# Three gathers to a PSUM bank, twelve places for gathered rows, steps of six, and fewer reports from TensorE

## What is computed

```
xn = layernorm(x)
W[r] = sum_b comp[r, b] * basis[b]                      # 8 relations, 4 bases
agg[dst] += xn[src] @ W[type]                            # over all edges
h = gelu(agg + xn @ loop_w + h_bias + xn)
gnn = layernorm(h) * gamma + beta
query, key = xn @ W_qk + b_qk;  value = xn @ W_v + b_v
lam = softmax(key over nodes)^T @ value;  mix = query @ batchnorm(lam)
x = x + gnn + mix
t = layernorm(x); e = argmax(t @ router_w^T + router_b)  # one of 32 experts
x = x + relu(relu(t @ W1[e] + b1[e]) @ W2[e] + b2[e])
```

## Time and profile before

| | us |
|---|---|
| median of 3 runs (lowest, highest) | 764.96 (764.16, 765.04) |
| profiled execution, its own time | 765.41 |
| its span, first to last instruction | 763.7 |
| mean granted TensorE clock | 0.903 of full |

### The profile page before, as it was taken

One profiled execution on the slowest core, in us unless ns is written; L12 is line 12 of the kernel. 1 busy time (PEld: TensorE's weight loads), 2 busy tenths in 40 slices (PEclk: granted clock), 3 DMA queues, 4 the chain that ended last, 5 costly groups with the idle time before them and its releaser, 6 DMA issues.

```text
span 763.7 us, 10470 instructions
## 1 busy us (share of the span) xinstructions
PE 602.2 (79%) x3189; PEld 474.0 (62%) x3189; DVE 381.1 (50%) x1267; ACT 167.1 (22%) x358; POOL 469.2 (61%) x480
## 2 busy tenths in 40 slices
PE   2577777888888877799999889987998895178980
PEld 1466666666666556676777668766867763166860
DVE  6534444223333324526566645657466566723652
ACT  3800000000000001102332312323223144135420
POOL 9667666666666666766666766677676600263265
PEclk9989996899999997699999989998999897579986
DMA  6643333332323334333444433444434316563021
GB/s 213 203 127 90 93 92 91 94 92 84 96 87 96 88 96 138 112 96 106 129 120 123 130 111 110 122 122 123 118 108 128 112 50 191 129 183 92 22 85 67
DMA packets 41873, 85.35 MB, mean 112 GB/s; under 512 B 11280, under 2 KB 23506, under 8 KB 41619
## 3 DMA queue, kind: packets, MB, share of 16 engines
q0 software_dynamic: 22576, 61.01, 27.4%
q1 hardware_dynamic: 18372, 22.95, 9.5%
q10 hardware_dynamic: 864, 0.65, 0.3%
HBM read 71.77 MB, written 12.80 MB: 111 GB/s over the span
## 4 chain that ended last, share of the span: by engine, by line
PE 43%; issue 16%; DVE 10%; POOL 10%; DMA 8%; another core or an unknown queue 5%; ACT 5%; DVEq 0%; ACTq 0%; POOLq 0%; SPq 0%
PE ps L846 22%; PE ps L904 7%; POOL gath L585 6%; DMA gath<-xn_d,src_i 5%; PE ps L893 3%; PE ps L873 2%; PE ps L1106 2%; POOL both L612 2%; DVE wmat L1241 2%; PE ps L1115 2%; POOL out L617 2%; DVE acc_raw L1265 1%; DMA both<-rows_d,inv_i 1%; PE ps L927 1%
## 5 line engine op out<-in xcount | busy, mean ns | idle before, releaser
L585 POOL DMA_INDIRECT gath<-xn_d,src_i x392 | 389.6, 994 | 191.0 <-issue 93.4
L846 PE MATMUL ps<-wmat,gath 128*128 128x144 f32 x1568 | 275.0, 315 | 53.3 <-DMA gath<-xn_d,src_i 25.6
L846 PEld LDWEIGHTS ps<-wmat,gath 128*128 128x128 f32 x1568 | 234.3, 206 | 93.0 <-issue 40.0
L1265 DVE TENSOR_TENSOR acc_raw<-acc_raw,ps 128x144 f32 x392 | 101.6, 300 | 276.4 <-PE ps L846 176.8
L1241 DVE TENSOR_TENSOR wmat<-hit,wts 128x576 f32<-128x576 f32 x100 | 75.3, 753 | 0.1
L612 POOL DMA_INDIRECT both<-rows_d,inv_i x25 | 24.3, 972 | 61.2 <-DVE inv_i L1514 49.1
L904 PE MATMUL ps<-wq_wv,acc_raw 128*128 128x256 f32 (+1 forms) x200 | 53.9, 389 | 2.8 <-issue 2.8
L904 PE MATMUL ps<-wk_et,acc_raw 128*128 128x256 f32 (+1 forms) x200 | 53.7, 392 | 0.9 <-issue 0.4
L893 PE MATMUL ps<-cmat,both 128*128 128x512 f32 (+1 forms) x100 | 47.2, 594 | 1.2 <-issue 1.1
L1560 DVE SCALAR_TENSOR_TENSOR acc_raw<-ps,wts,acc_raw 128x256 f32 x56 | 27.0, 482 | 41.2 <-PE ps L1115 28.6
L617 POOL DMA_INDIRECT out<-acc_raw,inv_i x25 | 25.8, 1032 | 34.2 <-DVE acc_raw L1551 28.1
(11 more groups left out here) (202 smaller groups left out, 616.7 us busy)
## 6 DMA issues: line engine op xcount, KB each, us to landing
gath<-xn_d,src_i POOLq DMA_INDIRECT x392
rows_d<-both SPq DMA_DIRECT2D x24, 256.0 KB
both<-in_x SPq DMA_DIRECT2D x24, 128.0 KB
both<-in_x SPq DMA_DIRECT2D x4, 640.0 KB, 9.8
xn_d<-both SPq DMA_DIRECT2D x4, 640.0 KB
acc_raw<-in_w_t SPq DMA_DIRECT2D x1, 2080.0 KB
acc_raw<-in_w_t SPq DMA_DIRECT2D x1, 2048.0 KB, 7.5
both<-in_x SPq DMA_DIRECT2D x1, 512.0 KB
```

Source lines behind the costliest of these rows:

```text
L585: g.indirect_dma_start(gath[:, k, :], None, xn_d, bass.IndirectOffsetOnAxis(ap=src_i[:, OCT * q + k:OCT * q + k + 1], axis=0)).then_inc(ga ...
L846: ins = t_.matmul(ps_edge[quarter][:, m * B * WIN:(m + 1) * B * WIN], gath[:, k, m * P:(m + 1) * P], wmat[:, k, :, :].rearrange("p b w -> ...
L1265: d.tensor_tensor(place, place, ps_edge[w][:, m * B * WIN:(m + 1) * B * WIN].rearrange("p (b w) -> p b w", w=WIN), ALU.add).then_inc(added, 1)
```

## The change

- A step ("sextet") has six columns in two triples instead of eight in four pairs; there are 65 steps (the last has seven columns) instead of 49. `gath` and `wmat` have RING = 12 places instead of 8.
- A triple has a whole PSUM bank: 8 groups (2 halves x 4 bases) of SPAN = 64 nodes. Each column keeps its own window of WIN = 22 nodes, at its own offset in the span. PE first clears the bank with a matmul of 512 bf16 columns of zeros, then each of the 3 x 2 products adds 4 runs of 22 numbers at an offset that PE has in a register (a register load for each step). DVE adds the whole bank, 512 columns, in one instruction for a triple.
- PE reports once for a triple (adding 3), once for both halves of a maximum, once for two keys, and once in all for the weighted sums.
- The table of bounds has bases of columns, offsets, bases of triples and a flag; it is stored in one transfer and loaded by four, `base_bc` in runs of six numbers for each partition. DVE computes it with about ten small operations.
- `STARTS` and the pieces' places in a step are laid out anew: two pieces after each triple. `ones_pp` and `reach` are made later.

```diff
-WIN = 36
-PAIR = 2
-OCT = 8
-NOCT = -(-E // (P * OCT))
-ETAB = (NOCT + 1) * OCT
+WIN = 22
+SPAN = 64
+THREE = 3
+SIX = 2 * THREE
+RING = 2 * SIX
+COLS = -(-E // P)
+NSIX = COLS // SIX
+NTRI = -(-COLS // THREE)
+ETAB = 432
-STARTS = [24, 25, 26, 27, 28, 29, 30, 31, 32, 34, 35, 36, 37, 38, 39, 40, 42, 43, 44, 45, 46, 47, 48]
+STARTS = [24, 25, 26, 28, 31, 34, 36, 39, 41, 43, 45, 47, 49, 50, 52, 54, 55, 57, 58, 60, 62, 63, 64]
...
-            sp.dma_start(base_bc, bounds_d[0:1, :].to_broadcast([P, NWIN])).then_inc(bounds_loaded, 16)
+            sp.dma_start(bounds_d, bounds[:, :]).then_inc(bounds_stored, 16)
+            sp.wait_ge(bounds_stored, 16)
+                sp.dma_start(base_bc.rearrange("p (r g) -> p r g", g=SIX),
+                              bounds_d[:, 0:SIX].rearrange("(a r) g -> a r g", a=1).to_broadcast([P, ROWS, SIX])).then_inc(bounds_loaded, 16)
...
+            def sextet(q, beside, i):
+                for c in [c for t3 in triples_of(q) for c in columns_of(t3)]:
+                    pool.wait_ge(multiplied, SIX + max(c - RING + 1, 0))
+                    g.indirect_dma_start(gath[:, c % RING, :], None, xn_d,
+                                         bass.IndirectOffsetOnAxis(ap=src_i[:, c:c + 1], axis=0)).then_inc(gathered[c % RING], 16)
...
+            def edges(t3, offsets):
+                bank = ps_edge[t3 % 4]
+                pe.wait_ge(added, t3 + 1)
+                t_.matmul(bank[:, :], onesb[0:1, :], identb[0:1, 1:2].to_broadcast([1, KD * B * SPAN]), start=True, stop=True)
+                pe.wait_ge(wmat_built, t3 + 1)
+                for c in columns_of(t3):
+                    pe.wait_ge(gathered[c % RING], 16 * (c // RING + 1))
+                    for m in range(KD):
+                        place = bank[:, :].rearrange("p (c n) -> p c n", n=SPAN)[:, m * B:(m + 1) * B, ds(offsets[c - THREE * t3], WIN)]
+                        ins = t_.matmul(place, gath[:, c % RING, m * P:(m + 1) * P], wmat[:, c % RING, :, :],
+                                        start=False, stop=True, skip_group_check=True)
+                ins.then_inc(multiplied, len(columns_of(t3)))
...
-                ins.then_inc(max_mult, 1)
+                if m == KD - 1:
+                    ins.then_inc(max_mult, KD)
...
-                t_.matmul(ps_mix[t % 2][0:n, 0:D], onesb[0:3, 0:n], shift3[:, :], start=False, stop=True).then_inc(keyed, 1)
+                if nth % 2 == 1:
+                    ins.then_inc(keyed, min(nth, 2))
...
-                ins.then_inc(summed, 1)
+                if nth == NT:
+                    ins.then_inc(summed, 1)
...
+                offsets = row_values(pe, off_row[0:1, cols[0]:cols[-1] + 1], SPAN - WIN, AN_OFFSET)
+                edges(2 * q, offsets[0:THREE])
+                piece(q, 0, beside, i)
+                piece(q, 1, beside, i)
+                edges(2 * q + 1, offsets[THREE:SIX])
...
+            def add_triple(t3, base):
+                v.wait_ge(multiplied, SIX + columns_of(t3)[-1] + 1)
+                v.wait_ge(added, t3 + 4)
+                place = acc[:, :, ds(base, SPAN)]
+                d.tensor_tensor(place, place, ps_edge[t3 % 4][:, :].rearrange("p (c n) -> p c n", n=SPAN), ALU.add).then_inc(added, 1)
```

More of the change, by code:

```diff
@@ L61 @@
 CLAMPED = "the pairs' experts and tiles are counts from zero, cut to the last expert and tile by a minimum before they are stored"
-A_NODE = "each base is the least node number among its edges, and acc has a row's width of columns beyond the last node"
+A_NODE = "each base is the least node number among its edges, and acc has a span of columns beyond the last node"
+AN_OFFSET = "each offset is a node number less the least of its triple, cut by a minimum to the last that leaves a gather's columns in the span"
 assert TS * TG == P and TS * TW == TC * P and KD * B * NPAD % ZEROS == 0
-assert OCT == 4 * PAIR and ETAB % ROWG == 0 and NT % GROUPS == 0 and PAIRS % 2 == 0
-assert STARTS[0] == CHAIN0 and len(STEP) == INLINE and INLINE == NT - 2 and STARTS[-1] == NOCT - 1
+assert NTRI == 2 * NSIX + 1 and ETAB % SIX == 0 and ETAB >= NTRI * THREE and KD * B * SPAN == 512 and N + SPAN <= NPAD + 1 and NT % GROUPS == 0 and PAIRS % 2 == 0
+assert STARTS[0] == CHAIN0 and len(STEP) == INLINE and INLINE == NT - 2 and STARTS[-1] == NSIX - 1
 assert NPAIR % FT == 0 and NPAIR <= P
@@ L82, in pairs_within, with triples_of, columns_of @@
     return [w for w in range(PAIRS + 1) if min(2 * w + 1, NT - 1) // GT == g]
+def triples_of(q):
+    return [2 * q, 2 * q + 1] + ([NTRI - 1] if q == NSIX - 1 else [])
+def columns_of(t3):
+    return range(THREE * t3, min(THREE * t3 + THREE, COLS))
 def runs_of_reach():
     seen, q = [], CHAIN0
-    while q < NOCT:
+    while q < NSIX:
         n = 1
-        while q + n < NOCT and q + n in STEP:
+        while q + n < NSIX and q + n in STEP:
             n += 1
-        seen.append((q - CHAIN0, n, sum(s <= q for s in STARTS)))
+        seen.append((2 * (q - CHAIN0), n, sum(s <= q for s in STARTS)))
         q += n
@@ L132, in gps_layer @@
         token = both[:, :].rearrange("p (t f) -> p t f", f=ROW)
[L133 to L135 removed]
+        gath = sb("gath", [P, RING, D])
+        wmat = sb("wmat", [P, RING, B, WIN])
+        hit = sb("hit", [P, THREE, WIN])
         rel = sb("rel", [P, ETAB])
@@ L576, in _ @@
                 zero_acc(i)
+            for first, n, count in runs_of_reach():
+                p_own.mark(g.iota(reach[:, first:first + 2 * n], pattern=[[P, n], [0, 2]], base=P * count, channel_multiplier=0))
+            p_own.mark(g.iota(reach[:, NTRI - 1 - 2 * CHAIN0:], pattern=[[0, 1]], base=P * INLINE, channel_multiplier=0))
+            pool.wait_ge(p_own.sem, p_own.at)
+            pool.sem_inc(consts_made, 1)
             pool.wait_ge(xn_stored, 16 * (GROUPS + 1))
@@ L1243, in build_weights @@
                                 ALU.mult).then_inc(wmat_built, 1)
-            for half in range(2):
-                build_hit(0, half)
-                build_weights(0, half)
+            for t3 in triples_of(0):
+                prepare(t3)
             v.wait_ge(acc_zeroed, ZEROS)
```

247 lines of the change are left out of this document (114 added, 133 removed).

## The result

The kernel after takes 777.97 us (median of 4 runs, 776.09 to 783.70) and the kernel before, on the same chip, 765.0. That is 1.0179 times as long (interval 1.0148 to 1.0209), so it is slower. The forecast was 749 us, a gain.

The account below looks back on a forecast made before the run. POOL's gathers were taken to set the pace, pausing for held-back TensorE reports, with PE second. 191.9 us around the stream + 11 for the table + 546.0 stream + 0.3 = 749 us; own range 735 to 762, over all cases 703 to 776.

Parts of the forecast that it names:

- Twelve places and triples: Gather stream: more places and fewer reports lengthen runs from 8.9 to 13 gathers, leaving 30 pauses of 1.87 us; -27.5 us.
- the 82.3 us: Gather stream of before: 573.5 us less 491.2 for 392 unhindered gathers at 1.253 us, all read as POOL's pauses.
- The delay grows with the run: Gather stream: POOL runs longer but every pause lasts longer too; stream stays at 565, 768 us in all; chance 0.08.
- The first rival: Gather stream: the number of reports causes the delay, so six pauses are left; 704 us; chance 0.25.
- some 600: TensorE's reports saved; at the skill's 26.3 ns each, worth 16 us at most, nothing where PE has slack.
- The second: Start: the table load is slower than estimated; at 150 pieces per us the time is 792 us; chance 0.12.
- the third: Edge products: strided output slows them, 0.150 us per product where weights need 0.11; 775 us; chance 0.13.
- The table: Start: loading `base_bc` as 9,216 pieces of 24 B delays the first gather to 49 us; +11, bounds 0 and +98.
- The ten small DVE operations ahead of it lie under the wait for x: 0: Start: DVE's table operations ahead of the first gather are hidden by the wait for x; cost 0.
- PE's stream: Edge products: the narrower window saves 20 us, zeroing matmuls add 29 to 57 at 0.22 to 0.44 each; cost 0.
- the 9 us more of PE's work: PE's net added work beside the gathers, taken as hidden at cost 0; it counts if that cover is gone.
- costed at 0.3 us: Near the end: `ones_pp` filled by DVE, 0.3 us, the only cost put behind the stream.

Follow-up runs that it names:

- the second pair of profiles: The kernels before and after, both unchanged, run again on a chip with late reports: 764.09 us and 776.28 us.
- `dense14`: The kernel after with a report for each gather and fourteen places of `gath` instead of twelve, on a late chip: 785.11 us, 1.0255 of before.
- `table`: The kernel after with bases, offsets and flags each stored in and loaded from a contiguous row, on a prompt chip: 685.64 us, 1.0040 of before.
- `before_pace`: The kernel before with POOL writing zeros to 160 columns of an unused tile behind each gather, on a prompt chip: 721.31 us, 1.0529 of before.
- `pace160`: The kernel after with POOL writing zeros to 160 columns of an unused tile behind each gather, on a prompt chip: 730.41 us, 1.0663 of before.
- the fillers: POOL zeroes unused columns behind each gather: 160 in before (721.31 us) and after (730.41), 320 in after (776.9, 774.49, 775.11).
- half gathers: The kernel after, from the thirteenth gather on, with 512 B pieces instead of 1,024 B (687.14 and 686.04 us) or 64 rows instead of 128 (681.42).

## Why the prediction was wrong

**Pauses read right, cause of their sum wrong.** The rows do show reports held back while POOL issues back to back, and POOL stopping for lack of one. The step that failed is "*Twelve places and triples*": "Runs go from 8.9 to 13 gathers, and 391 gathers have 30 pauses", -27.5 us. It took the pause as a fixed price per stop, to be paid less often with more places. Measured: 53 pauses, +4.9 us (+1.3 in the second pair of profiles; after's own two differ by 4.5, so a loss in the stream itself is not settled, only that there is no gain). The pace is 1.46 to 1.48 us per gather with 8, 12 or 14 places, and the pause is what it takes to get back to it. The numbers were in the profile of before: 573.5 / 392 is 1.463 from the earlier trace rows, and the 25 row gathers, with other waits, have 1.46 too. Also, the 82.3 us were not all pauses: the 392 gathers took 994 ns in the mean and not 950, 17 us in all. After lost these 17 us and its stream got no shorter, which a price per stop doesn't explain and a fixed pace does.

**The nearest rival had the smallest chance.** "The delay grows with the run", the stream stays at 565, 768 us, 0.08. Its mechanism is what the late chips show; its stream was 9 to 13 us too short, and the losses at the start and the end were not in it. The first rival (number of reports) is refuted by 53 pauses with a third of the edges' reports, and by `dense14`, whose stream with all of them (577.8) is as long as after's (578.4 and 573.9). (TensorE sends 678 reports in before and 368 in after, 310 fewer, not the "some 600" of the prediction; its bound of 16 us is halved by that, and nothing else.) The second fell with the first gather at 42.01, the third with the pitch.

**The table: +11 predicted, 0 measured.** The pieces go at 1,390 per us, where the estimate took 545 from SP's pace of issue for another load; and nothing waited for them (`table`). The prediction's own lower bound, 0, is what came.

**"The ten small DVE operations ahead of it lie under the wait for x: 0"** is the second step that failed: +3.9 us. They were taken to fit beside a wait for x, and no cause for a hold was looked for: three of them end only with POOL's fill, and the statistics stand behind them on DVE. The Trainium skill ("SBUF — State Buffer", SBUF: two separate sides) says that VectorE and GpSimd share a pair of ports as an exclusive lock, and that VectorE takes part in it in its two-port modes. The trace agrees: three tiny TENSOR_SCALAR operations end with POOL's fill (11.01 and 10.99), while a reduction inside the fill takes 0.15 us (`table`) and before's statistics run through it. No run moved the fill or the operations, so that the start would be 3.9 us earlier without this meeting is read from the timelines and not tested.

**PE's stream, right in its terms.** A pitch of 0.117 us at the upper level against 0.11, an addition of 0.686 against 0.69. The zeroing instruction takes 0.32 before the products start (411.84 to 412.16), between the bounds of 0.22 and 0.44 and above the 0.22 taken. The strided output behind a register costs a product next to nothing (0.117 where the weights need 0.11), against the rule weighed as the third rival, which had 0.150. What the terms left out is the clock: the 9 us more of PE's work became 43.2, of which 10.7 in the sums' window alone, at 0.85. From a gather's start to its first product it is 3.2 to 5.8 us (medians by stage) in before on the late chips and 8.7 to 13.5 in after.

**Behind the last gather**, costed at 0.3 us: the last product with the basis ends 23.5, 23.5 and 19.6 us after the last gather in before, 27.4 and 28.5 in after. With prompt reports and one pitch (`before_pace`, `pace160`) it is 19.7 against 24.3. This has two parts. From the last edge product to the last one with the basis it is 15.4 us in all four profiles of before and 17.2 in all 16 of kernels with the change, so these +1.8 us belong to the change on any chip. The rest is how far the last edge product trails the last gather: 8.1, 8.1 and 4.2 us in before, 10.2 and 11.3 in after, 4.3 against 7.1 with the fillers, and 3.1 to 4.5 in after once the pitch is 1.50. That the triples' products are behind because PE has more to do was only argued.

**Open.** What takes 1.46 us on the late chips, given that the rows arrive in time, and whether it counts bytes, rows or transfers: the fillers and half gathers met prompt chips only. Theory G describes the seven profiles, but no late chip tested it: that a POOL paced to 1.46 us would get its reports at once there was not shown. Nor was why the clock stays low in after, or how much of the loss it is on either kind of chip.

## What to carry to other kernels

Divide a stream's time by its transfers before you explain its pauses, and do it for each loop that issues the same kind. If loops with other waits and other numbers of places have one pace, more places only move the pauses. Small operations of VectorE are priced with what GpSimd runs at that time (4.39 us in place of some 0.15 here), and an edit of a last stage by what is left when the stream ends. Compare kernels on one chip only. Before a fix is built around a delay, see whether it is there on another chip.

## What the hardware showed unexpectedly

- Chips differ by 80 us of 765 for one and the same kernel. They differ in the mean pace of indirect transfers and in TensorE's reports: 1.46 us and up to 8 us late, or 1.25 and 14 ns. By the fillers the pace makes 68 of the 80 us.
- On the late chips the gathered rows arrive as soon as on the others, 1.46 us (median) after POOL's instruction, though TensorE's reports are late.
- A TENSOR_SCALAR on 72 x 1 numbers took 4.3 us beside a fill on POOL.
- The granted clock stayed at 1.2 GHz for 37.5 us (105.5 to 143.1 in after), in the last 19 of which TensorE had no idle time. The same twelve fp32 instructions took 2.86 us there and 1.57 at 2.4 GHz.
- With half of the rows a gather costs POOL 0.911 us in place of 0.958; with half of each row, 0.958.
